# Transposing attention's output with DMA transfers of SyncE's queue, and adding V's bias at V's eviction

## The reference

```python
Q = einsum('bse,hed->bhsd', x, Wq) + bq      # K and V likewise; 16 heads of 64
scores = einsum('bhsd,bhtd->bhst', Q, K) / 8
w = softmax(where(causal, scores, -inf))
o = einsum('bhst,bhtd->bhsd', w, V)          # then (b, s, 1024)
x = layernorm(x + o @ Wo + bo)
h = silu(x @ wg.T) * (x @ wu.T)              # hidden 3072, int weights / 127
x = layernorm(x + h @ wd.T)
```

## Time and profile before

| | us |
|---|---|
| time, median of three runs | 1165.81 (1165.63 to 1166.45) |
| the profiled execution's own time | 1166.87 |
| its span on the slowest core (core 2, role 0) | 1165.2 |
| its span on core 3 (role 1's slowest) | 1162.8 |
| PE busy, of the span of core 2 | 1118.3 |
| ACT busy | 602.1 |
| DVE busy | 390.9 |
| POOL busy | 87.9 |

### The profile page before, as it was taken

The page is one execution under the profiler, slowest core; times in us unless marked ns, Lnnn a source line. Parts: engine busy times, 40 slices in busy tenths (PEclk is TensorE's granted clock), DMA queues, the critical chain, the costliest instruction groups (busy, mean ns, idle before and its releaser), DMA issues.

```text
span 1165.2 us, 28546 instructions; the slowest of 8 cores (1160.5 to 1165.2 us)
## 1 busy us (share of the span) xinstructions
PE 1118.3 (96%) x11460; PEld 676.3 (58%) x11568; DVE 390.9 (34%) x833; ACT 602.1 (52%) x723; POOL 87.9 (8%) x156
## 2 busy tenths in 40 slices
PE   3899999999999999999999999999999999999997
PEld 1676677767676677765555566666444444444443
DVE  0333323333333433335667522222333212121333
ACT  0588889999999899898855411112000111111000
POOL 3000000000000000013010211111000111110000
PEclk9999999999999999999999999999999999999999
DMA  9902100021001103069655764334111345441011
GB/s 128 155 3 38 21 2 3 2 39 21 2 3 21 20 3 74 33 153 244 138 129 109 147 107 73 63 65 73 37 55 55 74 75 82 78 73 19 37 45 66
DMA packets 32200, 74.61 MB, mean 64 GB/s; under 512 B 3648, under 2 KB 9792, under 8 KB 31168
## 3 DMA queue, kind: packets, MB, share of 16 engines
q0 software_dynamic: 26448, 54.80, 28.4%
q1 hardware_dynamic: 5616, 17.91, 4.1%
HBM read 109.65 MB, written 8.91 MB: 102 GB/s over the span
## 4 chain that ended last, share of the span: by engine, by line
PE 93%; issue 2%; DMA 2%; DVE 2%; ACT 1%; POOL 0%; POOLq 0%; DVEq 0%; ACTq 0%
PE ps_s L850 15%; PE ps_s L856 15%; PE bank_o L826 11%; PE ps_s L794 11%; PE ps_s L767 10%; PE ps_u L697 7%; PE ps_u L716 7%; PE ps_u L708 5%; PE ps_u L767 5%; PE ps_u L732 4%; DMA x<-x 2%; PE ps_s L732 1%; PE bank_o L746 1%; ACT PT L897 1%; PE ps_s L753 0%
## 5 line engine op out<-in xcount | busy, mean ns | idle before, releaser
L897 ACT ACTIVATE PT<-ps_s 128x1024 bf16<-128x1024 f32 x510 | 490.2, 1024 | 56.0 <-PE ps_s L794 48.9
L911 ACT ACTIVATE gs<-ps_s 128x384 bf16<-128x384 f32 (+1 forms) x120 | 63.9, 533 | 260.3 <-PE ps_s L850 260.1
L850 PE MATMUL ps_s<-x1T,wgb 128*128 128x384 bf16 (+1 forms) x953 | 195.5, 347 | 0.4
L856 PE MATMUL ps_s<-x1T,wub 128*128 128x384 bf16 (+1 forms) x952 | 195.3, 347 | 0.4
L826 PEld LDWEIGHTS bank_o<-V,PT 128*128 128x128 bf16 x4080 | 155.8, 97 | 46.9 <-issue 23.1
L826 PE MATMUL bank_o<-V,PT 128*128 128x65 bf16 x4080 | 176.4, 193 | 2.4 <-DVE PT L1006 2.0
L794 PE MATMUL ps_s<-Q2T,K2T 64*128 64x256 bf16 (+1 forms) x2736 | 158.4, 244 | 4.0 <-ACT PT L897 1.5
L1028 DVE TENSOR_TENSOR hT<-ps_s,gs 128x384 bf16<-128x384 f32 (+1 forms) x120 | 73.3, 611 | 264.3 <-PE ps_s L856 252.7
L850 PEld LDWEIGHTS ps_s<-x1T,wgb 128*128 128x128 bf16 x960 | 93.8, 98 | 83.2
L856 PEld LDWEIGHTS ps_s<-x1T,wub 128*128 128x128 bf16 x960 | 93.9, 98 | 82.6
L767 PE MATMUL ps_s<-wd_sb,hT 128*128 128x512 bf16 x541 | 120.2, 379 | 0.6
(11 more groups left out here) (57 smaller groups left out, 599.2 us busy)
## 6 DMA issues: line engine op xcount, KB each, us to landing
wgb<-wg POOLq DMA_DIRECT2D x48, 256.0 KB, 4.1
wub<-wu POOLq DMA_DIRECT2D x48, 256.0 KB, 5.1
xq_sb<-bo SPq DMA_DIRECT2D x17, 512.0 KB, 5.2
xq_sb<-xq POOLq DMA_DIRECT2D x17, 512.0 KB, 11.1
y<-y SPq DMA_DIRECT2D x17, 512.0 KB, 2.7
wd_sb<-wd POOLq DMA_DIRECT2D x6, 1024.0 KB, 14.2
x<-x POOLq DMA_DIRECT2D x4, 1024.0 KB, 28.2
wk_sb<-wk POOLq DMA_DIRECT2D x8, 256.0 KB, 4.6
```

Of the source, the lines that this page charges most:

```text
L850: inst = pe.matmul(ps_s[w % 2][:, 0, 0:n], wgb[:, i % 4, ec, :], x1T[:, ec, q:q + n], start=(ec == 0), stop=(ec == NEC - 1))
L856: inst = pe.matmul(ps_s[w % 2][:, 1, 0:n], wub[:, i % 4, ec, :], x1T[:, ec, q:q + n], start=(ec == 0), stop=(ec == NEC - 1))
L897: act.activation(PT[:, no % NSLOT], ps_s[no % 3][:], AF.Exp, scale=SCALE).then_inc(sem_exp, 1)
L911: act.activation(gs[:, no % 2, 0:n], ps_s[no % 2][:, 0, 0:n], AF.Silu, scale=1.0 / 127.0).then_inc(sem_silu, 1)
```

## The change

PE's transposes of attention's output go, with the order entry 'O', the DVE eviction `rows_in` and `ps_t`. Instead SP transposes each 128x128 piece of `o_nat` by a transfer with `transpose=True` straight into `o_allT`, as soon as the division is done; the second block after waits for that before it writes the same buffer of `o_nat`. V's bias, which `rows_in` added, is now added where V leaves PSUM, by `tensor_add` with a bias tile of 512 KB in place of the copy.

SP's queue changes with it. Its `bo` transfers were first held until V's last projection. Now slots 2 and 3 are filled at the very beginning; slots 0, 1 and 4 stand behind the transposes of the first block of the last pair; slots 5 to 11 behind those of the first block that ends after the last K, Q or V unit; slots 12 and up behind the transposes of all blocks. POOL takes the slots in the order 2, 3, 0, 1, 4. W may start at another step.

```diff
@@ Plan @@
-        block = self.block_end.index(h)
-        if block:
-            self.pe.append(('O', block - 1))
-        return block
+        return self.block_end.index(h)
...
-            first = self.block_end[nb * (NPAIR - 1) + qt // 2 + 1] // (4 * STEP) + 5
+            first = self.block_end[nb * (NPAIR - 1) + qt // 2] // (4 * STEP) + 6
...
-            if qt == NROWS + 1:
-                self.pe.append(('O', nb - 1))
-                self.dve.append(('B', nb - 1))
...
+    def projected(self):
+        last = max(i for i, (what, a) in enumerate(self.pe)
+                   if what == 'U' and self.units[a[0]][0] in 'KQV')
+        place = {a: i for i, (what, a) in enumerate(self.pe) if what == 'P'}
+        return next(b for b, h in enumerate(self.block_end) if place[h] > last)
@@ SP @@
         def sync_program(sp):
-            for qt in range(role.nset):
-                if qt < 2:
-                    sp.wait_ge(sem_unit, plan.all_done('V', 3))
-                elif qt == 5:
+            def rows_in(b):
+                sp.wait_ge(sem_o, b + 1)
+                p, q, n = block_rows(b)
+                for i in range(n // 128):
+                    sp.dma_start(o_allT[:, p, q + 128 * i:q + 128 * i + 128], o_nat[:, b % 2, i, :],
+                                 transpose=True).then_inc(sem_ot[b % 2], 16)
+
+            for qt in (2, 3):
+                sp.dma_start(xq_sb[qt][:], d['bo']).then_inc(sem_bo[qt], 16)
+
+            v_done, x_done = 7 * nblock, plan.projected()
+            for b in range(NPAIR * nblock):
+                rows_in(b)
+                if b == v_done:
+                    sp.wait_ge(sem_ev, plan.all_done('V', 3))
+                    for qt in (0, 1, 4):
+                        sp.dma_start(xq_sb[qt][:], d['bo']).then_inc(sem_bo[qt], 16)
+                if b == x_done:
                     sp.wait_ge(sem_unit, plan.all_done('K', 7))
                     sp.wait_ge(sem_unit, plan.all_done('Q', 7))
-                elif qt >= 12:
-                    sp.wait_ge(sem_ev, plan.done('W', xq_slot(qt), 1))
+                    for qt in range(5, 12):
+                        sp.dma_start(xq_sb[qt][:], d['bo']).then_inc(sem_bo[qt], 16)
+            for qt in range(12, role.nset):
+                sp.wait_ge(sem_ev, plan.done('W', xq_slot(qt), 1))
                 sp.dma_start(xq_sb[xq_slot(qt)][:], d['bo']).then_inc(sem_bo[xq_slot(qt)], 16)
@@ POOL @@
-            for qt in range(5):
+            for qt in (2, 3, 0, 1, 4):
                 add_rows(qt)
...
-            pool.wait_ge(sem_tr, NPAIR * nblock)
             load_gu(4)
+            for i in range(2):
+                pool.wait_ge(sem_ot[i], ot_count(...))
@@ PE: block_out is removed; rows_out waits for @@
+                    if qt < 2:
+                        pe.wait_ge(sem_ot[(b - 1) % 2], ot_count(b - 1))
+                    pe.wait_ge(sem_ot[b % 2], ot_count(b))
@@ DVE, eviction of V @@
-                    dve.tensor_copy(V2[...], ps[...])
+                    if unit == ('V', 0, 0):
+                        dve.wait_ge(sem_bv, 16)
+                    dve.tensor_add(V2[...], ps[...], bv_sb[:, a] broadcast over the chunks)
@@ DVE, normalised(b) @@
-                    dve.wait_ge(sem_tr, b)
+                dve.wait_ge(sem_pv, plan.pv_count[plan.block_end[b]])
                 dve.reciprocal(...)
-                if b:
-                    rows_in(b - 1)
+                if b >= 2:
+                    dve.wait_ge(sem_ot[b % 2], ot_count(b - 2))
                 dve.tensor_mul(o_nat[:, b % 2, 0:n], ...)
@@ start of SP's program, behind four small constants @@
+            sp.dma_start(bv_sb[:], d['bv']).then_inc(sem_bv, 16)
```

More of the change, by code:

```diff
@@ L108, in __init__ @@
         self.tiles = [range(h, min(h + 4, n)) for h in range(0, n, 4)]
+        ends = sorted({t[-1] for t in self.tiles} | set(self.block_end))
+        self.pv_count = {h: i + 1 for i, h in enumerate(ends)}
         self.steps = -(-len(self.tiles) // STEP)
@@ L367, in _network @@
     def _network(self):
-        role, nb = self.role, len(self.block_end)
+        role = self.role
         ring = itertools.cycle((0, 2, 1))
@@ L487, in build @@
     sem_pv = sem('sem_pv')
-    sem_block = sem('sem_block')
+    sem_bv = sem('sem_bv')
     sem_rec = sem('sem_rec')
     sem_o = sem('sem_o')
-    sem_tr = sem('sem_tr')
-    sem_ot = sem('sem_ot')
+    sem_ot = [sem(f'sem_ot{i}') for i in range(2)]
     sem_bn = sem('sem_bn')
@@ L525, in build @@
     mask_sb = place('mask_sb', 206.25, [128, 128], BF16)
+    bv_sb = place('bv_sb', 199.5, [128, 4, 256], F32)
     rec = place('rec', 206.5, [128, 2, 2, 2], F32)
-    bv_sb = place('bv_sb', 206.65625, [128, NPAIR], F32)
     bq_sb = place('bq_sb', 206.6875, [128, NPAIR], F32)
@@ L579, in block_rows, with ot_count @@
             return b // nblock, *role.blocks[b % nblock][:2]
+        def ot_count(b):
+            return 16 * sum(block_rows(i)[2] // 128 for i in range(b % 2, b + 1, 2))
         def sync_program(sp):
-            for qt in range(role.nset):
-                if qt < 2:
-                    sp.wait_ge(sem_unit, plan.all_done('V', 3))
-                elif qt == 5:
+            def rows_in(b):
[14 more added lines that the diff above has]
+                if b == x_done:
                     sp.wait_ge(sem_unit, plan.all_done('K', 7))
                     sp.wait_ge(sem_unit, plan.all_done('Q', 7))
-                elif qt >= 12:
-                    sp.wait_ge(sem_ev, plan.done('W', xq_slot(qt), 1))
+                    for qt in range(5, 12):
+                        sp.dma_start(xq_sb[qt][:], d['bo']).then_inc(sem_bo[qt], 16)
+            for qt in range(12, role.nset):
+                sp.wait_ge(sem_ev, plan.done('W', xq_slot(qt), 1))
                 sp.dma_start(xq_sb[xq_slot(qt)][:], d['bo']).then_inc(sem_bo[xq_slot(qt)], 16)
@@ L727, in rows_out @@
                     pe.wait_ge(sem_wo, 16)
-                if nblock * 7 + qt // 2 + 1 > seen_ot:
-                    seen_ot = nblock * 7 + qt // 2 + 1
-                    pe.wait_ge(sem_ot, seen_ot)
+                b = nblock * 7 + qt // 2
+                if b >= seen_ot:
+                    seen_ot = b + 1
+                    if qt < 2:
+                        pe.wait_ge(sem_ot[(b - 1) % 2], ot_count(b - 1))
+                    pe.wait_ge(sem_ot[b % 2], ot_count(b))
                 for hdc in range(first, last):
@@ L735, in rows_out @@
                 return inst
[L737 to L747, removed]
             def transposed(qt, ps):
@@ L829, in products @@
                                      stop=plan.diagonal(h), skip_group_check=True)
-                if h == plan.block_end[0]:
-                    inst.then_inc(sem_block, 1)
-                if h == plan.tiles[m][-1]:
+                if h in plan.pv_count:
                     inst.then_inc(sem_pv, 1)
@@ L884, in tensor_program @@
                     products(no)
-                elif what == 'O':
-                    block_out(no)
                 else:
@@ L895, in scalar_program @@
                     if no >= NSLOT:
-                        act.wait_ge(sem_pv, no - NSLOT + 1)
+                        act.wait_ge(sem_pv, plan.pv_count[plan.tiles[no - NSLOT][-1]])
                     act.activation(PT[:, no % NSLOT], ps_s[no % 3][:], AF.Exp,
@@ L926, in project @@
                     c = plan.v_chunks(unit)
[L927 to L937, removed]
+                    if unit == ('V', 0, 0):
+                        dve.wait_ge(sem_bv, 16)
+                    dve.tensor_add(V2[:, a % 2, c[0]:c[-1] + 1, :, 0:64],
+                                   ps[:, 0:256 * len(c)].rearrange("p (c h f) -> p c h f", h=4, f=64),
+                                   bv_sb[:, a].rearrange("p (h f) -> p h f", f=64).unsqueeze(1)
+                                   .broadcast_to([128, len(c), 4, 64])).then_inc(sem_ev, 1)
             def normalised(b):
-                if b:
-                    dve.wait_ge(sem_tr, b)
-                else:
-                    dve.wait_ge(sem_block, 1)
+                dve.wait_ge(sem_pv, plan.pv_count[plan.block_end[b]])
                 n = block_rows(b)[2] // 128
                 dve.reciprocal(rec[:, b % 2, 0:n], ps_o[:, 0:n, :, 64]).then_inc(sem_rec, 1)
-                if b:
-                    rows_in(b - 1)
+                if b >= 2:
+                    dve.wait_ge(sem_ot[b % 2], ot_count(b - 2))
                 dve.wait_ge(sem_rec, b + 1)
```

16 lines of the change are left out of this document (7 added, 9 removed).

## The result

The changed kernel takes 1189.74 us (median of four runs) against 1165.81: the ratio is 1.0201, 95% interval 1.0181 to 1.0221, so some 23 us slower. One of the four runs fell in a slow state of the chip, at 1376.84 us, and the ratio leaves it out; the other three took 1188.66 to 1190.09. Forecast were 1164.2 and a range of 1160 to 1170.

What follows compares the result with a forecast made beforehand. PE's queue was taken as the bound. On core 2, PE's saving of 7.3 us, 3.5 us of later start and 2.2 us for slot 0 sum to -1.6, from 1165.81 to 1164.2 us; range 1160 to 1170.

Steps and rivals of the forecast that it cites:

- PE's saving: Transposes leaving PE's queue, 0.054 us each: 7.3 us saved on role 0, 6.5 us on role 1.
- DVE: Dropped evictions of transposed rows (24 us) and V's copy turned into an addition (694 to 692 ns): worth nothing.
- the sum: Core 2: -7.3 + 3.5 + 2.2 = -1.6 us, span 1163.6; core 3: span 1160.2, no longer than core 2.
- The start: Bias tile and bo for slots 2 and 3 load before x: PE's start 3.5 us later, between 2.0 and 4.8.
- the gap: Some 2.2 us of free DMA between 3 and 7 us, taken to hold most of the first added load.
- Slot 0: First slot of xq_sb ready late for the first W eviction: PE delayed 2.2 us on role 0, 0.4 on role 1.
- The transfers' own delay: Divisions waiting for transposing transfers of the second block before: two issues and 3.0 us just fit 3.9; nothing taken.
- third rival: Transposes land late at role 1's short blocks, deciding from 5.9 us: 2.1 x 8 = 17 us on core 3; chance 0.15.

Runs made afterwards that it cites:

- experiment 2: The kernel before with each of PE's transposes of attention's output done twice: ratio 1.0044, 5.1 us slower.
- experiment 1: The kernel before with only V's bias moved to V's eviction, its 512 KB tile loaded at the start, PE's transposes kept: ratio 1.0013.
- experiment 5: The changed kernel with bo for slots 2 and 3 issued behind the transposes of pair 2's fourth block, not at the start: 1186.6 us.
- Experiment 6: The changed kernel with bo for slots 0, 1 and 4 behind the first block that ends after the last V unit: 1186.04 us.
- Experiments 3 and 4: The changed kernel: Wo and first additions issued after the transposes of pair 6's third block, 1178.21 us; or four o_nat buffers for two, 1176.34 us.
- experiment 11: The kernel before, unchanged, run once more for its trace on the chip of these runs: 1166.48 us.
- experiment 12: The changed kernel with four o_nat buffers, Wo and first additions later, bo transfers moved or spread, only 128 KB of bias at the start: 1163.46 us.
- experiment 9: The changed kernel with two o_nat buffers, Wo and first additions later, bo transfers moved or spread, only 128 KB of bias at the start: 1164.98 us.
- experiment 8: The changed kernel with Wo loaded by four transfers of 256 columns in place of one of 1024: ratio 1.0153.

## Why the prediction was wrong, step by step

**PE's saving: right in kind, a quarter too large.** 7.3 us were forecast for role 0 from the chain's 0.11 us a pair. Doubling costs 5.1 us (3.4 to 6.8), and the stretches between reciprocals of experiment 2 give 0.043 us for one, 5.9 us in all. For role 1 they give less than the 6.5 that were forecast: the four-buffer kernel, whose core 3 waits for no transpose, needs 358.97 us from block 7 to block 47 where before needs 361.88, so 0.039 us each for 75 and 4.7 for 120. The start is no place to read it from: core 2 came out of its wait there at half clock before (0.50 from 28 to 30 us) and at the full one after.

**DVE: right.** Row of the kernel after, core 3 (54 evictions of V; core 2 has the 48 of the sum):

```profile
L938 DVE TENSOR_TENSOR V<-ps_u,bv_sb 128x512 bf16<-128x512 f32 x54 | 37.4, 693 | 105.6 <-PE ps_u L737 105.6
```

**The start: right in kind, too small.** 3.5 us were taken; the middle of the eight cores moved by 4.2 to 4.8 (27.5 or 28.1 to 32.3), within the bounds of 2.0 to 4.8. What failed is that the first transfer "falls into the gap for the most part": the bias tile alone costs 1.5 us (experiment 1). Nor did the two bo transfers follow it at once: they were issued at 7.5 us on core 2, and on core 3 here,

```profile
L595 SPq DMA_DIRECT2D xq_sb<-bo x2: 337/552/766, 13.9 to 14.3; - x2
```

in the full stretch. They cost 2.2 to 3 us of start (experiment 5).

**Slot 0: right in kind, too small, above all on role 1.** PE waits 3.9 us on core 2 and 4.2 on core 3, where 2.2 and 0.4 were forecast. The sum took 0.46 us for each issue of SP, but a transposing issue takes 1.1 to 1.2 us. The chain of core 3 after, from block 56's transposes to the eviction:

```profile
606.37 1.08 SPq L591
...
607.49 1.20 SPq L591
...
608.78 5.06 DMA xq_sb<-bo
...
614.37 7.80 DMA xq_sb<-xq
...
622.27 0.70 DVE y L971
```

4.25 us had been taken from bo's issue to POOL's and 7.0 for the landing; they are 5.6 and 7.8. The issues add 1.5 us, so the three make 3.7 us of the 3.8 that were missing on core 3. Experiment 6 takes the wait away.

**The transfers' own delay: wrong, and this step decides.** The text says "I take nothing". The landing time itself was guessed well: 3.0 us was used, 2.6 is the median, and besides the wait of 11.6 us and one of 2.8 right behind it, DVE on core 3 has three of 1.4 to 2.0 us, block 58's among them. What was left out is a transposing transfer beside a large one. The traffic was looked at for bo in SP's own queue and, through a mean share of 0.09 in a stretch far off, for "seven of the eight pairs"; the eighth, in which POOL sends Wo exactly as the short blocks come, wasn't followed. 15 to 16 us to land there is far past the 5.9 us from which the third rival was to decide. Experiments 3 and 4 remove the wait from its two ends, by moving the load and by giving the division another buffer, and each gives back 11 to 14 us of the time. So the third rival was the one that came true, with 0.15. Its mechanism was right, its place nearly: a division of role 1 waits for the block two before it, but the long wait is block 49's for block 47, not one of the short block 58 for 56. Its count was wrong: it was to be 8 times 2 us, and was once 10.9 us of PE with small ones beside. That its 17 us lie near the 15.4 of that stretch is luck.
Role 0 has its own. The text called transposes behind three bo transfers harmless, the block that needs them being "two blocks and 10 us or more away", and didn't look at the seven behind block 65. The transposes of block 66 stand behind those seven and take 22.6 us; block 68 wants the buffer 18.6 us after block 66's division and waits 5.3 us (chain of core 2 after):

```profile
548.65 1.10 SPq L591
...
549.79 22.58 DMA o_allT<-o_nat
572.42 0.05 issue
...
572.53 0.44 DVE o_nat L952
```

**A term that the sum didn't have: the clock behind a stall.** PE works at half clock for 9 us behind the long wait and for 5 us behind slot 0's. That costs some 7 us on core 3 (4.5 and 2.5, estimates: half of those times), more than the transposes ever could give back. The sum took each stall at its own length.

**Another term that it didn't have: the end of role 0.** When the last rows of y have landed, SP has only its closing instructions left. Its last waits for those landings, and then its drain at the end of the program, core 2 before and core 2 after:

```profile
L597 SPq EVENT_SEMAPHORE  x3: 17/17/17, 1162.1 to 1164.8; - x3
L1035 SPq DRAIN  x1: 7/7/7, 1165.0 to 1165.0; - x1
...
L617 SPq EVENT_SEMAPHORE  x3: 17/17/17, 1176.9 to 1179.3; - x3
L1034 SPq DRAIN  x1: 50/50/50, 1181.9 to 1181.9; - x1
```

From the last wait to the drain it is 0.2 us before and 2.6 us after. Every kernel here whose SP transposes shows this on all four cores of role 0: the span ends 2.9 to 3.2 us after y's last landing, where the kernels without it (before, experiments 1, 2 and 11) have 0.5 to 0.6. Role 1, whose program stands last in SP's, has 0.3 to 0.4 in all of them. So with SP's transposes role 0 pays some 2.5 us at its end, in the experiments too. Why SP needs that time was not tested.

**The sum afterwards for core 3**, from the events: start 3.5; up to the end of pair 5 the saving of 90 transposes at most (3.5 us at 0.039) against PE waits of 1.9 us and a longer stretch at half clock behind the start, -0.1; pair 6's Wo 15.4; slot 0 4.2; the rest, half clock mostly, 2.7: 25.7.

**What stays open.** With all causes on the list away the gain is 2.2 to 2.7 us, on role 0, which then ends last. There PE's saving is 5.9; the end takes back 2.5, and the start, against the 28.1 us of experiment 11, some 0.3 in experiment 12 and 1.3 in experiment 9 (this one on another chip). That leaves 3.1 and 2.1 us, within the intervals (1.5 to 3.7 and 1.0 to 3.4). What SP does in the 2.5 us is open, and why a small transfer lands so late beside a large one is shown only in part (experiment 8).

## What to carry to other kernels

A transfer that takes work from PE must be costed where it is slowest, beside the largest transfer that can be under way when somebody waits for it; list for each wait what the other queues send in those microseconds. Where the wait is for a buffer to come free, more buffers or a moved load cure it alike. A stall of a busy PE was dearer than its length here, since PE came out of it at half clock. And the price of an instruction is read best from a long stretch between two equal events, with the instruction there, doubled and gone, and not from the busy time or one place in the chain.

## What the hardware showed that I had not expected

- A transposing transfer of 128x128 bf16 between two places of SBUF costs SP 1.08 to 1.2 us to issue (a plain one of 32 KB 0.4) and lands in 2.2 us at the least, in 2.6 in the middle, in 14.9 to 16.4 beside 3 MB of POOL's transfers and in 22.6 behind and beside bo's and POOL's. Two of them count as 320 packets and 0.07 MB in the queue (core 3, 404 to 412 us).
- PE, busy before, stood idle from 522.3 to 533.2 us; its granted clock was 0.50, that is 1.2 GHz, from 526 to 542 us, so through 9 us of work behind the stall. A stall of 4.2 us had 0.50 from 622 to 628 us behind it.
- SP issued the first transfers behind its role branch at 7.5 us on core 2 and 13.9 us on core 3, though bv's load before the branch went out at 2.9 us. On core 3 the branch itself stands at 7.2 us.
- SP's program with 136 transposes and their waits in role 0 came to its drain 2.6 us behind its last wait on core 2, the one without them 0.2 us.
- A transpose of 128x128 on PE, 218 ns long in the trace, cost 0.043 us in PE's full queue on core 2, whether it was added or taken away.
